# An expert layer's down product with weights stationary, its bias added by VectorE and its result transposed back by TensorE

## The chip, the core and the metric

The kernel runs on one core of a Trainium2 chip. A core has a matrix engine (TensorE; in the profile PE for its matmuls and PEld for its weight loads), VectorE (DVE), ScalarE (ACT), GpSimd (POOL) and SyncE (SP, which here issues DMAs). Each engine takes its own instructions in order, and they wait for one another by semaphores. TensorE multiplies a stationary operand, loaded as weights, with a moving one, and writes to PSUM, eight banks of 2 KB per partition; the other engines' data lie in SBUF, with 128 partitions. The metric is the device time of one execution in microseconds, lower being better.

## What is computed

Two layers, each with an attention and a mixture of experts, on 2 x 1024 tokens of 128 channels. The change lies in the experts of the first layer: a router picks one of 16 experts for each token, and the expert is a small two-layer network with biases.

```python
def _L0_ffn_ref(h, router_w, w1, b1, w2, b2):
    B, S, D, F, E = (2, 256, 128, 256, 16)
    b, s, d = h.shape
    x = h.reshape(-1, d)
    logits = x @ router_w
    assign = jnp.argmax(logits, axis=-1)
    w = jax.nn.sigmoid(jnp.take_along_axis(logits, assign[:, None], axis=1)[:, 0])
    hh = jnp.einsum('nd,edf->nef', x, w1) + b1
    hh = jax.nn.gelu(hh, approximate=False)
    all_out = jnp.einsum('nef,efd->ned', hh, w2) + b2
    out = jnp.take_along_axis(all_out, assign[:, None, None], axis=1)[:, 0, :]
    out = out * w[:, None]
    return out.reshape(b, s, d)
...
x = L0_attn_x
h = _layernorm(x, axis=-1) * (1 + ca) + sa
x = x + ga * _L0_attn_ref(h, ...)
h = _layernorm(x, axis=-1) * (1 + cb) + sb
x = x + gb * _L0_ffn_ref(h, ...)
...
```

The second layer (another attention, another set of experts) follows on `x`.

## The kernel before

The program has three phases, one after the other, with an exit of all engines between them: `rwkv_phase` (the first attention; it also routes the tokens and scatters their rows to `moe0_slots` in DRAM, sorted by expert), `expert_phase` (the experts of the first layer), and `layer1_phase`.

`expert_phase` works on 31 tiles of 128 rows: 16 that belong to one expert each and 15 more for rows that were over, whose expert is looked up. A tile goes through these steps:

- SyncE loads the rows (`xg`), TensorE transposes them into PSUM (`transpose`, L1453), and VectorE copies them to SBUF (`inputs`, L1422).
- TensorE makes the up product in two halves of 128 hidden units (`up`, L1462), weights stationary. The hidden units lie on the partitions, so ScalarE adds the first bias per partition as it applies the gelu (L1399) and writes `hid`.
- TensorE makes the down product (`down_product`). Before the change `hid` is the stationary operand and the weights move (L1469), so the tokens lie on the partitions of the result, as the store wants them. The second bias then varies along the free dimension; it is added by a third matmul, the bias column broadcast against the identity (L1471), accumulated into the same PSUM tile.
- VectorE copies the result from PSUM to `yg` (`results`, L1426), and SyncE stores `yg` to `moe0_slots` in eight groups of tiles (L1372), the last of three tiles. GpSimd waits for all stores and then gathers the first tokens' rows for the next phase (L1315).

All is written as a pipeline by hand: in round n TensorE transposes tile n+2, makes the up product of tile n and the down product of tile n-3; VectorE copies the inputs of tile n+2 and the results of tile n-3. Rounds run from -2 to 33, so the first rounds have no down product, rounds 29 and 30 no transpose, and the last three only a down product. A tile uses one of `DEPTH` = 8 PSUM banks: columns 0 to 255 hold the up product, 256 to 383 the transposed input (`tr`), 384 to 511 the down product (`down`). Tile n+8 may be transposed into a bank when the results of tile n have been copied.

After the loop TensorE runs 14 fillers (L1483) that keep it busy while the last results are stored; then each engine leaves the phase (L1322), and `layer1_phase` starts when all have.

Of the kernel before, what the change touches and what calls it, by code (L numbers as in the profile page):

```python
# [18 lines left out]
ALU = mybir.AluOpType  # L19
# [3 lines left out]
P = 128  # L23
# [15 lines left out]
E0, F0 = 16, 256  # L39
# [5 lines left out]
W0 = 2 * F0 + 3  # L45
# [66 lines left out]
def bass_adaln_stack(nc, t, out):  # L112

    ctx = ExitStack()
    with ctx:
# [64 lines left out]
        with nc.sbuf_tensor("hT_all", [P, TILES, P], F32) as hT_all:  # L180
            with nc.cleanup_on_exit():
                expert_phase(nc, t, const, bank + halves, cst, wall, s_wall, h_all, ends0, s_sent0, mx0,
                             gate, gate_rows, s_gate, yt, weight, slot0, s_back)
                layer1_phase(nc, t, const, x_sb, x_bc, eps_pow, sbw[:, 1], mod_col, mod_row, quad, bank, pair, cst,
                             hT_all, W1, s_w1, s_w2, s_fill, gate_rows, yt, weight, slot0, s_back, wall, h_all,
                             out)
# [1132 lines left out]
def expert_phase(nc, t, const, bank, cst, wall, s_wall, h_all, ends, s_sent, mx, gate,  # L1319
                 gate_rows, s_gate, yt, weight, slot, s_back):  # L1320

    with ExitStack() as ctx:  # L1322
        def sb(name, shape, dt=F32):
            return ctx.enter_context(nc.sbuf_tensor(name, shape, dt))

        def sem(name):
            return nc.alloc_semaphore(name)

        ALL = E0 + EXTRA0
        DEPTH = len(bank)  # L1330
# [9 lines left out]
        hid = [sb(f"e_hid{k}", [P, 2, P]) for k in range(DEPTH)]  # L1340
        yg = sb("e_yg", [P, ALL, C])
# [4 lines left out]
        s_out = sem("e_s_out")  # L1346
        e_xt, e_xc, e_up, e_gelu, e_down, e_y = (sem("e_s_xt"), sem("e_s_xc"), sem("e_s_up"), sem("e_s_gelu"),
                                                 sem("e_s_down"), sem("e_s_y"))
        s_grow, s_growc = sem("e_s_grow"), sem("e_s_growc")
        block = ctx.enter_context(nc.Block())  # L1350

        def tr(k):
            return bank[k][:, 2 * P:3 * P]

        def down(k):
            return bank[k][:, 3 * P:4 * P]

        def weights(n):
            return wall[:, n, :] if n < E0 else wdyn[:, n - E0, :]
# [42 lines left out]
        @block.vector  # L1402
        def _(dve):
            for k in range(len(BATCHES)):
                dve.tensor_tensor(le[:, :, k, :], ends[0:1, k, None, 1:].to_broadcast([1, EXTRA0, E0]),
                                  cst("iota15")[0:1, :, None].to_broadcast([1, EXTRA0, E0]), ALU.is_le).then_inc(s_step, 1)
            dve.wait_ge(s_step, len(BATCHES))
            dve.tensor_reduce(te[:, :], le[:, :, :, :].rearrange("p d k e -> p d (k e)"), AX.X, ALU.add)\
                .then_inc(s_step, 1)
            dve.wait_ge(s_step, len(BATCHES) + 1)  # L1410
            dve.tensor_copy(expert[:, :], te[:, :]).then_inc(s_step, 1)
            dve.wait_ge(s_step, len(BATCHES) + 2)
            dve.tensor_scalar(expert[:, :], expert[:, :], E0 - 1, None, ALU.bitwise_and).then_inc(s_tile, 1)

            dve.wait_ge(s_exp, 1)
            dve.tensor_scalar(weight[:, :], weight[:, :], 1.0, None, ALU.add).then_inc(s_exp, 1)
            dve.wait_ge(s_exp, 2)
            dve.reciprocal(weight[:, :], weight[:, :]).then_inc(s_exp, 1)

            def inputs(n):  # L1420
                dve.wait_ge(e_xt, n + 1)
                dve.tensor_copy(xgT[n % DEPTH][:, :], tr(n % DEPTH)).then_inc(e_xc, 1)  # L1422

            def results(n):
                dve.wait_ge(e_down, n + 1)
                dve.tensor_copy(yg[:, n, :], down(n % DEPTH)).then_inc(e_y, 1)  # L1426

            for n in range(-2, ALL + 3):
                if n + 2 < ALL:
                    inputs(n + 2)  # L1430
                if n >= 3:
                    results(n - 3)

        @block.tensor
        def _(pe):
            pe.wait_ge(s_gate, 16)
            for e in range(E1_LIVE):
                last = pe.matmul(bank[6][:, e * C:(e + 1) * C], gate[:, e:e + 1].to_broadcast([P, P]), cst("ident"),
                                 start=True, stop=True)
            last.then_inc(s_grow, 1)  # L1440
            for _ in range(3):
                pe.matmul(bank[5][:, 0:2 * P], cst("ident"), const[:, 0:2 * P], start=True, stop=True)

            def transpose(n):
                if n < E0:
                    pe.wait_ge(s_x[[b > n for _, b in LOADS].index(True)], 16)
                else:
                    pe.wait_ge(s_x[len(LOADS) + [b > n - E0 for _, b in OVER].index(True)], 16)
                if n >= DEPTH:
                    pe.wait_ge(e_y, n - DEPTH + 1)  # L1450
                if n == 6:
                    pe.wait_ge(s_growc, 1)
                pe.transpose(tr(n % DEPTH), xg[:, n, :], cst("ident")).then_inc(e_xt, 1)  # L1453

            def up(n):
                pe.wait_ge(e_xc, n + 1)
                if n == 0:
                    pe.wait_ge(s_wall, 16)
                if n >= E0:
                    pe.wait_ge(s_wt[n - E0], 16)  # L1460
                for f in range(2):
                    last = pe.matmul(bank[n % DEPTH][:, f * P:(f + 1) * P], weights(n)[:, f * P:(f + 1) * P],  # L1462
                                     xgT[n % DEPTH][:, :], start=True, stop=True)
                last.then_inc(e_up, 1)

            def down_product(n):
                pe.wait_ge(e_gelu, 2 * n + 2)
                for f in range(2):
                    pe.matmul(down(n % DEPTH), hid[n % DEPTH][:, f, :], weights(n)[:, F0 + f * P:F0 + (f + 1) * P],  # L1469
                              start=(f == 0), stop=False)  # L1470
                pe.matmul(down(n % DEPTH), weights(n)[:, W0 - 1:W0].to_broadcast([P, P]), cst("ident"), start=False,  # L1471
                          stop=True).then_inc(e_down, 1)

            for n in range(-2, ALL + 3):
                if n + 2 < ALL:
                    transpose(n + 2)
                if 0 <= n < ALL:
                    up(n)
                if n >= 3:
                    down_product(n - 3)  # L1480
            pe.wait_ge(e_y, ALL - 1)
            for _ in range(14):
                pe.matmul(bank[0][:, 0:2 * P], cst("ident"), const[:, 0:2 * P], start=True, stop=True)  # L1483
# [1128 lines left out]
```

## Time and profile before

| | us |
|---|---|
| median of 3 runs | 685.11 (685.09 to 685.81) |
| the profiled execution | 684.28 |
| its span in the profile | 682.2 |
| of it, the loop over the expert tiles from round 4 on | 204.29 to 239.19 |
| TensorE busy in the span | 641.0 (94%) |
| VectorE busy | 421.7 (62%) |
| ScalarE busy | 302.7 (44%) |
| GpSimd busy | 254.8 (37%) |

The span is the time from the first to the last instruction of the profiled execution; 2.1 us of the execution lie around it. Times inside the profile are counted from the start of the span. A busy TensorE is not one at its peak, since its matmuls overlap and their ends are modelled: the distance from one weight load to the next tells its pace better. An instruction's idle time before it, with what ended it, stands in square brackets in the rows below.

### The profile page before, as it was taken

What the parts mean: (1) busy time and instruction counts of PE and PEld (TensorE: products, weight loads), DVE (VectorE), ACT (ScalarE), POOL (GpSimd) and SP (SyncE); (2) the same over time, 40 slices, a digit from 0 to 9 for tenths busy, and PEclk for the clock granted to TensorE, in tenths of its full rate; (3) what the DMA queues carried; (4) which work ended last, traced back from release to release, by engine and by line L of the source; (5) the groups of instructions that cost most, each with busy time, mean ns of one, the idle gap of its engine ahead of it and who ended that gap; (6) DMA issues with size and microseconds to landing.
All of it is one profiled execution on the core that took longest, in us unless ns stands there. A gap on an engine that the chain in (4) does not pass through costs nothing.

```text
span 682.2 us, 26441 instructions
## 1 busy us (share of the span) xinstructions
PE 641.0 (94%) x10978; PEld 547.5 (80%) x10978; DVE 421.7 (62%) x1384; ACT 302.7 (44%) x1017; POOL 254.8 (37%) x387
## 2 busy tenths in 40 slices
PE   5899999999759989999999999999999999999995
PEld 4567777777649977888888888888887999989995
DVE  3777777777633326577777686868676554444442
ACT  1456666643025414545545554545454353333331
POOL 1455666556710031131525252524243432322325
PEclk9899999999969999999999999999999999999999
DMA  7899200000048210000000000000221667566462
GB/s 191 287 299 308 57 3 2 4 6 19 25 137 244 82 43 7 7 9 7 20 12 20 14 18 16 16 16 12 97 77 26 225 223 240 186 214 225 154 241 62
DMA packets 50486, 65.69 MB, mean 96 GB/s; under 512 B 5168, under 2 KB 40208, under 8 KB 47424
## 3 DMA queue, kind: packets, MB, share of 16 engines
q1 hardware_dynamic: 44992, 57.22, 26.8%
q0 software_dynamic: 2912, 6.03, 2.6%
q8 instruction: 88, 1.44, 0.9%
q10 hardware_dynamic: 2464, 0.76, 0.5%
q14 instruction: 30, 0.25, 0.1%
HBM read 49.45 MB, written 18.87 MB: 100 GB/s over the span
## 4 chain that ended last, share of the span: by engine, by line
PE 59%; DVE 2%; DMA 1%; ACT 1%; issue 0%; SPq 0%; DVEq 0%
PE bank L1924 7%; PE quad L1782 6%; PE quad L1906 6%; PE quad L1908 5%; PE bank L1807 4%; PE pair L1744 3%; PE bank L1830 3%; PE quad L1788 2%; PE pair L1746 2%; PE pair L1745 2%; PE bank L1840 2%; PE pair L1769 2%; PE bank L1843 2%; PE bank L1833 2%; PE bank L1926 1%; PE quad L1911 1%
## 5 line engine op out<-in xcount | busy, mean ns | idle before, releaser
L2183 DVE TENSOR_TENSOR h_masked<-quad,const 128x1536 f32<-128x1536 f32 (+2 forms) x66 | 112.6, 1706 | 59.9 <-PE quad L1788 54.1
L2021 ACT ACTIVATE f_sa<-quad 128x256 f32<-128x256 f32 (+1 forms) x115 | 40.3, 352 | 91.6 <-PE quad L1908 75.8
L2202 DVE TENSOR_TENSOR f_hid<-f_sa,quad 128x256 f32<-128x256 f32 (+1 forms) x115 | 43.1, 380 | 53.6 <-ACT f_sa L2021 53.5
L2403 POOL DMA_INDIRECT moe_slots<-g_pay,g_slot x28 | 28.9, 1034 | 77.2 <-PE bank L1852 68.7
L1924 PE MATMUL bank<-wall,f_hid 128*128 128x128 f32 x390 | 50.7, 277 | 1.1 <-DVE f_hid L2205 0.9
L1924 PEld LDWEIGHTS bank<-wall,f_hid 128*128 128x128 f32 x390 | 47.8, 192 | 3.6 <-DVE f_hid L2205 2.8
L1906 PE MATMUL quad<-f_xT,wall 128*128 128x256 f32 (+1 forms) x190 | 50.0, 345 | 0.5 <-DVE f_hid L2202 0.5
L1908 PE MATMUL quad<-f_xT,wall 128*128 128x256 f32 (+1 forms) x190 | 49.2, 341 | 0.0
L1998 ACT ACTIVATE h_gT<-bank 128x128 f32<-128x128 f32 x64 | 17.8, 278 | 66.2 <-PE bank L1833 66.2
L1782 PE MATMUL quad<-h_qk 32*128 32x128 f32 x1024 | 46.5, 296 | 0.3 <-DVE h_masked L2183 0.3
L1782 PEld LDWEIGHTS quad<-h_qk 32*128 32x128 f32 x1024 | 34.3, 185 | 9.5 <-issue 7.0
L1807 PE MATMUL bank<-h_qk,h_state 32*32 32x128 f32 x1024 | 40.9, 274 | 0.0
L1972 ACT ACTIVATE h_qk<-pair 128x256 f32<-128x256 f32 x64 | 24.6, 384 | 36.1 <-PE pair L1746 36.1
L2483 POOL DMA_INDIRECT moe_out<-f_y,f_token x31 | 30.3, 977 | 23.9 <-DVE f_y L2311 16.5
L837 POOL TENSOR_TENSOR kl<-kl,tot 128x128 f32<-128x128 f32 x56 | 25.1, 449 | 33.6 <-DVE state L725 10.6
L1132 PE MATMUL bank<-const 128*128 128x256 f32 x134 | 35.1, 398 | 0.9 <-DVE sbw L479 0.9
L1908 PEld LDWEIGHTS quad<-f_xT,wall 128*128 128x128 f32 x190 | 33.4, 191 | 3.1
L1906 PEld LDWEIGHTS quad<-f_xT,wall 128*128 128x128 f32 x190 | 31.4, 191 | 3.5 <-issue 1.0
L1744 PE MATMUL pair<-hT_all,hla_wq 128*128 128x128 f32 x128 | 29.8, 315 | 0.7 <-ACT h_vt L1974 0.7
L1807 PEld LDWEIGHTS bank<-h_qk,h_state 32*32 32x32 f32 x1024 | 23.7, 104 | 7.7
L1981 ACT ACTIVATE h_kqt<-pair 128x256 f32<-128x256 f32 x64 | 24.8, 387 | 9.3 <-PE pair L1769 9.3
L1132 PEld LDWEIGHTS bank<-const 128*128 128x128 f32 x134 | 24.2, 194 | 4.2 <-DVE mod_row L471 1.3
(414 smaller groups left out, 1791.2 us busy)
## 6 DMA issues: line engine op xcount, KB each, us to landing
wall<-moe_w SPq DMA_DIRECT2D x23, 1088.0 KB, 5.1
moe_slots<-blank SPq DMA_DIRECT2D x2, 2112.0 KB, 24.4
wall<-in_experts_dram SPq DMA_DIRECT2D x1, 4120.0 KB, 21.8
e_w<-in_experts_dram SPq DMA_DIRECT2D x15, 257.5 KB, 3.3
moe_slots<-blank SPq DMA_DIRECT2D x1, 1984.0 KB, 9.7
moe_slots<-e_yg SPq DMA_DIRECT2D x7, 256.0 KB, 3.7
f_xg<-moe_slots SPq DMA_DIRECT2D x12, 132.0 KB, 4.1
moe_w<-in_moe_w_dram SPq DMA_DIRECT2D x1, 1408.0 KB, 7.2
```

The source lines that it names most:

```text
L1132: pe.matmul(bank[of][:, 0:N], cst("ident"), const[:, 0:N], start=True, stop=True)
L1744: pe.matmul(proj[:, 0:P], W["q"][:, cols], hT, start=True, stop=True)
L1782: last = pe.matmul(quad[:, h, a * P:(a + 1) * P], qk[q][head(h), 1 - a, :], qk[q][head(h), a, :], start=True, stop=True, tile_position=(h ...
L1807: pe.matmul(left[head(h), part * P:(part + 1) * P], states[k][head(h), (0 if part else 2 * D):(D if part else 3 * D)], qk[k][head(h), 1 - ...
L1906: pe.matmul(up_bank(n, f)[:, 0:s], w[:, F1 + TAIL1 + f * P:F1 + TAIL1 + (f + 1) * P], x_of(n)[:, 0:s], start=True, stop=True)
L1908: pe.matmul(up_bank(n, f)[:, T1:T1 + s], w[:, f * P:(f + 1) * P], x_of(n)[:, 0:s], start=True, stop=True).then_inc(f_up, 1)
L1924: pe.matmul(acc[k], hid[n % 2][:, f, cols], w[:, 2 * F1 + f * C:2 * F1 + (f + 1) * C], start=(f == 0), stop=False)
L2021: act.activation(sa[g % 3][:, 0:s], up_bank(n, f)[:, 0:s], ACT.Silu).then_inc(f_sa, 1)
L2183: dve.tensor_tensor(masked[k % 4][:, :, a * P:z * P], quad[:, :, a * P:z * P], cst("causal")[:, None, a * P:z * P].to_broadcast([P, HPG, ( ...
L2202: dve.tensor_tensor(hid[n % 2][:, f, 0:s], sa[g % 3][:, 0:s], up_bank(n, f)[:, T1:T1 + s], ALU.mult)\
L2403: pool.indirect_dma_start(out=t["moe1_slots"], out_offset=bass.IndirectOffsetOnAxis(ap=slot[:, b * 2 + k:b * 2 + k + 1], axis=0), in_=pay[ ...
L2483: pool.indirect_dma_start(out=t["moe1_out"], out_offset=bass.IndirectOffsetOnAxis(ap=token_of[n % 2][:, k:k + 1], axis=0), in_=yg[n % 2][: ...
```

## The change

The operands of the down product change places: the weights are stationary and `hid` moves, so the result has the output channels on the partitions and the tokens along the free dimension. The third matmul goes away. VectorE adds the second bias per partition as it takes the result out of PSUM (`biased`, into one of three buffers `yT`), TensorE transposes that back (`turn`) into the columns 0 to 127 of the same bank, which the up product has left, and VectorE copies it to `yg` as before. Two semaphores are new. The loops have one more round: in round n TensorE turns tile n-4 ahead of the down product of tile n-3, and VectorE copies the results of tile n-4 ahead of the bias of tile n-3.

```diff
--- before.py
+++ after.py
@@ -1346,6 +1346,8 @@
         s_out = sem("e_s_out")
         e_xt, e_xc, e_up, e_gelu, e_down, e_y = (sem("e_s_xt"), sem("e_s_xc"), sem("e_s_up"), sem("e_s_gelu"),
                                                  sem("e_s_down"), sem("e_s_y"))
+        yT = [sb(f"e_yT{k}", [P, P]) for k in range(3)]
+        e_biased, e_turned = sem("e_s_biased"), sem("e_s_turned")
         s_grow, s_growc = sem("e_s_grow"), sem("e_s_growc")
         block = ctx.enter_context(nc.Block())
 
@@ -1354,6 +1356,9 @@
 
         def down(k):
             return bank[k][:, 3 * P:4 * P]
+
+        def turned(k):
+            return bank[k][:, 0:P]
 
         def weights(n):
             return wall[:, n, :] if n < E0 else wdyn[:, n - E0, :]
@@ -1421,15 +1426,24 @@
                 dve.wait_ge(e_xt, n + 1)
                 dve.tensor_copy(xgT[n % DEPTH][:, :], tr(n % DEPTH)).then_inc(e_xc, 1)
 
+            def biased(n):
+                dve.wait_ge(e_down, n + 1)
+                if n >= 3:
+                    dve.wait_ge(e_turned, n - 2)
+                dve.tensor_scalar(yT[n % 3][:, :], down(n % DEPTH), weights(n)[:, W0 - 1:W0], None, ALU.add)\
+                    .then_inc(e_biased, 1)
+
             def results(n):
-                dve.wait_ge(e_down, n + 1)
-                dve.tensor_copy(yg[:, n, :], down(n % DEPTH)).then_inc(e_y, 1)
-
-            for n in range(-2, ALL + 3):
+                dve.wait_ge(e_turned, n + 1)
+                dve.tensor_copy(yg[:, n, :], turned(n % DEPTH)).then_inc(e_y, 1)
+
+            for n in range(-2, ALL + 4):
                 if n + 2 < ALL:
                     inputs(n + 2)
-                if n >= 3:
-                    results(n - 3)
+                if n >= 4:
+                    results(n - 4)
+                if 3 <= n < ALL + 3:
+                    biased(n - 3)
 
         @block.tensor
         def _(pe):
@@ -1466,17 +1480,22 @@
             def down_product(n):
                 pe.wait_ge(e_gelu, 2 * n + 2)
                 for f in range(2):
-                    pe.matmul(down(n % DEPTH), hid[n % DEPTH][:, f, :], weights(n)[:, F0 + f * P:F0 + (f + 1) * P],
-                              start=(f == 0), stop=False)
-                pe.matmul(down(n % DEPTH), weights(n)[:, W0 - 1:W0].to_broadcast([P, P]), cst("ident"), start=False,
-                          stop=True).then_inc(e_down, 1)
-
-            for n in range(-2, ALL + 3):
+                    last = pe.matmul(down(n % DEPTH), weights(n)[:, F0 + f * P:F0 + (f + 1) * P],
+                                     hid[n % DEPTH][:, f, :], start=(f == 0), stop=(f == 1))
+                last.then_inc(e_down, 1)
+
+            def turn(n):
+                pe.wait_ge(e_biased, n + 1)
+                pe.transpose(turned(n % DEPTH), yT[n % 3][:, :], cst("ident")).then_inc(e_turned, 1)
+
+            for n in range(-2, ALL + 4):
                 if n + 2 < ALL:
                     transpose(n + 2)
                 if 0 <= n < ALL:
                     up(n)
-                if n >= 3:
+                if n >= 4:
+                    turn(n - 4)
+                if 3 <= n < ALL + 3:
                     down_product(n - 3)
             pe.wait_ge(e_y, ALL - 1)
             for _ in range(14):
```

In the rows below an instruction is given as its line, its operation, the tile that it writes, those that it reads (the moving one first), and the shape; "x2" is two of them. `quad`, `pair`, `bank6` and `bank7` are PSUM. First TensorE in the middle of the loop, two rounds, before: L1453 is the transpose, L1462 the up product, L1469 and L1471 the down product and its bias.

```order
L1453 MATMUL quad<-const,e_xg 128x128
L1462 MATMUL quad<-e_xgT1,e_w 128x128 x2
L1469 MATMUL pair<-e_w,e_hid6 128x128 x2
L1471 MATMUL pair<-const,e_w 128x128
L1453 MATMUL bank6<-const,e_xg 128x128
L1462 MATMUL quad<-e_xgT2,e_w 128x128 x2
L1469 MATMUL pair<-e_w,e_hid7 128x128 x2
L1471 MATMUL pair<-const,e_w 128x128
```

The same two rounds on TensorE after: L1467 is the transpose, L1476 the up product, L1489 the turn, L1483 the down product.

```order
L1467 MATMUL quad<-const,e_xg 128x128
L1476 MATMUL quad<-e_xgT1,e_w 128x128 x2
L1489 MATMUL bank7<-const,e_yT0 128x128
L1483 MATMUL pair<-e_hid6,e_w 128x128 x2
L1467 MATMUL bank6<-const,e_xg 128x128
L1476 MATMUL quad<-e_xgT2,e_w 128x128 x2
L1489 MATMUL pair<-const,e_yT1 128x128
L1483 MATMUL pair<-e_hid7,e_w 128x128 x2
```

The bias matmul after the down product is gone; between the up product and the down product stands the turn of the tile whose down product ended the round before.

TensorE at the end of the loop, before (L1483 here is the fillers):

```order
L1462 MATMUL pair<-e_xgT6,e_w 128x128 x2
L1469 MATMUL quad<-e_w,e_hid3 128x128 x2
L1471 MATMUL quad<-const,e_w 128x128
L1469 MATMUL bank6<-e_w,e_hid4 128x128 x2
L1471 MATMUL bank6<-const,e_w 128x128
L1469 MATMUL bank7<-e_w,e_hid5 128x128 x2
L1471 MATMUL bank7<-const,e_w 128x128
L1469 MATMUL pair<-e_w,e_hid6 128x128 x2
L1471 MATMUL pair<-const,e_w 128x128
L1483 MATMUL quad<-const 128x256 x14
```

And after (the fillers are L1502):

```order
L1476 MATMUL pair<-e_xgT6,e_w 128x128 x2
L1489 MATMUL quad<-const,e_yT2 128x128
L1483 MATMUL quad<-e_hid3,e_w 128x128 x2
L1489 MATMUL quad<-const,e_yT0 128x128
L1483 MATMUL bank6<-e_hid4,e_w 128x128 x2
L1489 MATMUL bank6<-const,e_yT1 128x128
L1483 MATMUL bank7<-e_hid5,e_w 128x128 x2
L1489 MATMUL bank7<-const,e_yT2 128x128
L1483 MATMUL pair<-e_hid6,e_w 128x128 x2
L1489 MATMUL pair<-const,e_yT0 128x128
L1502 MATMUL quad<-const 128x256 x14
```

Down products and turns alternate, each turn directly behind the down product of its own tile, and one more turn stands at the end.

VectorE at the same place, before (L1422 copies inputs, L1426 results):

```order
L1426 COPY e_yg<-pair 128x128
L1422 COPY e_xgT5<-bank7 128x128
L1426 COPY e_yg<-quad 128x128
L1422 COPY e_xgT6<-pair 128x128
L1426 COPY e_yg<-quad 128x128 x3
L1426 COPY e_yg<-bank6 128x128
```

And after (L1427 copies inputs, L1438 turned results, L1433 adds the bias):

```order
L1427 COPY e_xgT5<-bank7 128x128
L1438 COPY e_yg<-pair 128x128
L1433 TENSOR_SCALAR e_yT0<-quad,e_w 128x128
L1427 COPY e_xgT6<-pair 128x128
L1438 COPY e_yg<-quad 128x128
L1433 TENSOR_SCALAR e_yT1<-quad,e_w 128x128
L1438 COPY e_yg<-quad 128x128
L1433 TENSOR_SCALAR e_yT2<-quad,e_w 128x128
```

A bias add has come into each round, behind the copy of the tile before it.

## Rows read from the trace of the kernel before

**Rows 1.** Busy us by stretch: length, TensorE, weight loads, VectorE, ScalarE, GpSimd, granted clock, DMA.

```profile
204.29:234.94 30.65, 30.65 (x278) 30.65 (x276) 12.21 (x50) 15.66 (x52) 0.00 (x0) 1.00 0.64 185
234.94:237.18 2.24, 2.24 (x23) 2.24 (x22) 0.58 (x2) 1.26 (x6) 0.00 (x0) 1.00 0.01 3
237.18:239.19 2.01, 2.01 (x21) 2.01 (x20) 0.88 (x3) 0.26 (x2) 0.00 (x0) 1.00 0.23 68
```

**Rows 2.** Order of time in one round: start us, us of the group, engine, instruction.

```profile
215.88 0.53 PEld L1469 LDWEIGHTS quad<-wall,e_hid 128*128 128x128 f32 x4
...
216.33 0.30 PEld L1471 LDWEIGHTS quad<-const,wall 128*128 128x128 f32 x2
...
216.55 0.14 PEld L1453 LDWEIGHTS quad<-const,e_xg 128*128 128x128 f32 x1
...
216.86 0.29 DVE L1426 COPY e_yg<-quad 128x128 f32<-128x128 f32 x1 [0.74 <-PE quad L1471]
217.07 0.28 DVE L1422 COPY e_xgT<-quad 128x128 f32<-128x128 f32 x1
```

**Rows 3.** Order of time, the first round with a down product.

```profile
203.63 0.53 PEld L1469 LDWEIGHTS quad<-wall,e_hid 128*128 128x128 f32 x4
...
204.07 0.30 PEld L1471 LDWEIGHTS quad<-const,wall 128*128 128x128 f32 x2
```

**Rows 4.** Order of time, the end of the loop.

```profile
238.96 0.30 PEld L1471 LDWEIGHTS pair<-const,e_w 128*128 128x128 f32 x2
...
239.19 0.73 PEld L1483 LDWEIGHTS quad<-const 128*128 128x128 f32 x4
...
239.49 0.29 DVE L1426 COPY e_yg<-pair 128x128 f32<-128x128 f32 x1 [0.38 <-PE pair L1471]
239.81 0.36 SPq L1372 DMA_DIRECT2D moe_slots<-e_yg  x1
```

**Rows 5.** Order of time from the last store to layer 1.

```profile
242.12 0.99 POOL L1315 DMA_INDIRECT e_yt<-moe_slots,slot_of_token  x1 [49.07 <-DMA moe_slots<-e_yg]
...
246.30 0.35 DVE L2040 SCALAR_TENSOR_TENSOR e_yt<-e_yt,router_weight,mod_row 128x128 f32<-128x128 f32 x1 [6.51 <-PEq L1322]
```

**Rows 6.** The exits of two engines: count, duration ns, start us.

```profile
L1322 PEldq DRAIN  x1: 4050/4050/4050, 241.5 to 241.5; - x1
L1322 POOLq DRAIN  x1: 4117/4117/4117, 241.9 to 241.9; - x1
```

**Rows 7.** VectorE by line and shape: count, busy us, mean ns, idle before.

```profile
L2311 DVE TENSOR_SCALAR f_y<-bank,f_xg 128x128 f32<-128x128 f32 x31 | 10.8, 350 | 21.5 <-PE bank L1926 21.5
...
L2057 DVE TENSOR_SCALAR p_xn<-x_sb,p_mv,p_rstd 128x128 f32<-128x128 f32 x16 | 4.9, 366 | 3.2 <-POOL p_rstd L2364 3.1 <-DVE g_cum L2067 0.2
L1426 DVE COPY e_yg<-quad 128x128 f32<-128x128 f32 x16 | 4.7, 292 | 12.1 <-PE quad L1471 12.1
```

**Rows 8.** Order of time at two hand-overs from VectorE to TensorE in layer 1.

```profile
301.12 0.48 DVE L2075 BATCH_NORM_STATS2 g_st<-x_sb 128x6 f32<-128x128 f32 x2
...
301.69 0.12 PEld L1807 LDWEIGHTS bank<-h_qk,h_state 32*32 32x32 f32 x4
...
566.57 0.41 DVE L2205 TENSOR_TENSOR f_hid<-f_sa,quad 64x256 f32<-64x256 f32 x1
...
567.03 0.19 PEld L1924 LDWEIGHTS bank<-wall,f_hid 128*128 128x128 f32 x1 [0.22 <-DVE f_hid L2205]
```

**Rows 9.** TensorE alone by stretch: length, busy us, granted clock, DMA share, GB/s.

```profile
198.20:200.90 2.70, 2.70 (x8) 0.50 0.94 273
...
244.00:248.00 4.00, 2.13 (x10) 1.00 0.07 21
```

**Rows 10.** Fillers by line and shape: count, busy us, mean ns of one.

```profile
L1483 PE MATMUL quad<-const 128*128 128x256 f32 x28 | 6.2, 379 | 0.0
...
L1442 PE MATMUL bank<-const 128*128 128x256 f32 x6 | 2.8, 634 | 0.0
```

## The prediction

> **What bounds the kernel now.** I read the busy times by stretch first. From 204.29 to 239.19 us, the loop over the 31 expert tiles, TensorE is busy all the time at a granted clock of 1.00; VectorE and ScalarE are busy 12.2 and 15.7 us of the first 30.65 [rows 1]. TensorE is what limits this stage. The 25 full rounds of the loop (a transpose, an up product, a down product with its bias) take 30.65 us, 1.226 us each. A round has 11 TensorE records: 1 of the transpose, 4 of the up product, 4 of the down product, 2 of the bias (a float32 matmul leaves two records, a transpose one), and so a record takes **p = 0.1115 us**. Then come two rounds without a transpose, 2.24 us, and three of down product and bias alone, 2.01 us [rows 1].
>
> Second, the order of time inside a round. The weight loads follow one another without a gap: down product at 215.88, bias at 216.33, next transpose at 216.55. The second load of the bias therefore stands at 216.33 + p = 216.44, and VectorE starts to copy the result at 216.86: **0.42 us** from the last weight load of a product to the start of the operation that reads it [rows 2]. At the end of the loop it is the same: 238.96 + p = 239.07, and the copy starts at 239.49 [rows 4]. Today this delay costs TensorE nothing, because nothing on TensorE waits for what VectorE made of a result, except a transpose several rounds later.
>
> Third, what follows. The last copy (239.49) lets SyncE store the last three tiles (239.81), the landing lets GpSimd gather (242.12), and layer 1 starts on VectorE at 246.30, when all engines have left the expert phase [rows 4, 5]. GpSimd leaves at 241.9 + 4.1 = 246.0, TensorE, behind its fillers, at 241.5 + 4.05 = 245.5 [rows 6]. So the end of the loop is on the path that sets the end, by way of GpSimd, and TensorE's fillers are 0.5 us behind. I see nothing later that starts by itself and could take up a shift: DMA engines are busy 7% of the time from 244 to 248 us [rows 9], and the gathers, the residual and the projections hang on one another.
>
> **The change, part by part.** *Operands of the down product exchanged*: 4 records as before, now of the up product's form (weights stationary, activations moving); both have pitch p inside the same rounds [rows 1, 2], so 0. A tile's down product comes three rounds after its up product, so the wait for its gelus stays met.
>
> *Bias matmul out, turn in.* Two records go, one transpose record comes, p less per tile: 31 x 0.1115 = 3.46 us, if TensorE never waited. That is the most the change can give.
>
> *New wait.* Now TensorE's turn of a tile needs the biased tile from VectorE, and VectorE needs the down product. Between the last load of the down product of a tile and the load of its turn lie: 0.42 us until VectorE starts [rows 2]; the bias add; and the hand-over to TensorE's weight load. The bias add is a VectorE TENSOR_SCALAR of 128x128 float32 from PSUM with a scalar per partition; the kernel has exactly this form in layer 1, 31 times at **0.350 us**, while a plain copy takes 0.292 [rows 7]. The hand-over from VectorE to a waiting weight load: the instruction that began at 566.57 and took 0.41 ended at 566.98, the load started at 567.03: **0.05 us** [rows 8]. Together L = 0.42 + 0.35 + 0.05 = **0.82 us**. The bias add has a second wait (its buffer, a turn three tiles older), long met.
>
> The Trainium skill, "VectorE: DVE Perf Modes", in the section on the TRN2 errata, gives one cost for any VectorE operation from PSUM to SBUF (120 cycles and one per element at 0.96 GHz, an estimate of 0.258 us here), and its table of perf modes puts copy and scalar operation into one row. By it the bias add would cost what a copy costs; the rows show 0.350 against 0.292, and I go by the rows. With the page's 0.258 us the sum below would be about +0.8 us instead of +3.7.
>
> What lies under L? TensorE goes in order: after the down product of a tile it does the next round's transpose (p) and up product (4p), then comes to the turn. That is 6p = 0.67 us from the last load of the down product, so in a full round it waits 0.82 - 0.67 = 0.15 us. And behind the waiting turn stands the next down product, on which the next turn hangs. That closes a loop: turn, down product, result to VectorE, bias, back to the turn. Its length is p for the turn's load, 3p to the last load of the down product after it, and L: **4p + 0.82 = 1.266 us per tile**, whatever else is in the round. It holds for the rounds without a transpose and, above all, for the last three, in which there is nothing to lie under the wait.
>
> VectorE can follow: 0.28 + 0.29 + 0.35 = 0.92 us per round [rows 2, 7]. It takes the copy of the turned tile 0.42 us after the turn's load and is done by 0.71; the next bias add can't start before 3p + p + 0.42 = 0.87. So the bias add isn't queued behind a copy. Transposes wait for copies two rounds older, and slack remains. ScalarE's load per tile stays, with more time for it. The weight loads of SyncE's queue only get more time; its stores are late as the results are.
>
> **The sum.** The first down product starts where it did, 203.63, its last load at 203.63 + 3p = 203.96 [rows 3]; there is no turn in that round. Before, the last bias load of tile 0 came 2p = 0.22 us later and that of tile 30 34.90 us after that (30.65 + 2.24 + 2.01), at 239.07. Now the turn of tile 0 is loaded at 203.96 + 0.82 = 204.78 and that of tile 30 at 204.78 + 30 x 1.266 = 242.76. Piece by piece: tile 0, 0.82 - 0.22 = +0.60; 25 full rounds, each 0.04 longer, +1.00; two rounds without transpose, 2.53 for 2.24, +0.29; three last rounds, 3.80 for 2.01, +1.79. **Together +3.7 us.** The saved record is in it already; the wait takes it back in each round, and the drained end costs 1.8 us on top. From there both are alike: copy 0.42 us after the load, store, gather, exit. TensorE's fillers wait for the copy of the last tile but one, met by then, and start 3.7 us later as well.
>
> The profiled execution took 684.28 us (span 682.2), which would become 688.0. The median of the runs is 685.11, 0.8 above it; I forecast **688.8 us**, +0.54%.
>
> Bounds: the bias add between the copy's 0.29 and the 0.37 of the dearest VectorE scalar operation of this size [rows 7]; the hand-over between 0.05 and the 0.09 of another, from 301.12 + 0.48 to 301.69 [rows 8]. L counts 31 times (30 rounds and tile 0). Low: 31 x 0.06 less, +1.8. High: 31 x 0.06 more, +5.6. A gain is excluded as long as L stays over 0.70 (below).
>
> **Rivals.**
> 1. *The wait is covered, TensorE alone sets the pace* (not slower). It decides by L: if L is at most 6p = 0.67, each round is 10p = 1.115 us to the end, tile 30 is turned at 203.96 + 0.67 + 30 x 1.115 = 238.08, and the change is 238.08 - 239.07 = -1.0 us: 684.1. Break-even is L = 0.70. For it: all three terms come from other instructions than the new ones. Against it: the 0.42 us is seen at every tile, and with 0.05 for the hand-over the bias add would have to take 0.23 us, less than any copy of that size [rows 7]. Chance 0.06 with what lies between.
> 2. *The clock falls* (slower still). In the last rounds TensorE has 5 records in 1.266 us, 0.56 us of load pitch, for about 4 us. If that counts as too little, the fillers run at 1.2 GHz: records of the same form have a mean of 634 ns at clock 0.50 and 379 at 1.00, with a pitch of (2.8 - 0.63)/5 = 0.43 against (6.2 - 0.38)/27 = 0.216 us [rows 9, 10]; 28 x 0.21 = 5.9 us, less the 0.5 us of slack: 694.2. Against: from 244.00 to 248.00 TensorE is busy 2.13 of 4 us, and the clock stays 1.00 there [rows 9]. Chance 0.04. The Trainium skill, "TensorE: Matmul & The Clock Gate", Part 4 on the PE-mode transpose, says that transposes don't engage the full clock as matmuls do, and one record in five would be one here; in the trace the loop with one in eleven stays at 1.00 [rows 1], which decides nothing for one in five.
> 3. *The shift is swallowed behind the loop.* If something else than the last copy released layer 1, TensorE's or GpSimd's exit would be late by less: 685.1. Against: GpSimd's gather waits for the landing of the store, and its exit is the last [rows 5, 6]. Chance 0.03.
>
> **How the numbers follow.** Forecast 0.87, rivals 0.06, 0.04, 0.03. The range is that of the forecast's bounds, 685.11 + 1.8 = 686.9 to 685.11 + 5.6 = 690.7; outside lie the rivals, 13 in 100, and a little of the forecast's own tails. A measurement of this kernel can tell about 0.2%, 1.4 us, from no change. Slower by more than that: the forecast and rival 2, 0.91. Within: rival 3 and most of rival 1, 0.07. Faster by more: it would need nearly all waits hidden, 0.02.
>
> **What would show it.** In the profile after: bias adds of 0.35 us; the weight load of the turn idle before it, released by VectorE, some 0.15 us in full rounds, 0.26 in the two without a transpose and 0.7 in the last; tiles 1.27 us apart from the first to the last, ends included; the last copy of results at 243.2; layer 1 from about 250.0, and after that everything shifted alike. TensorE busy without a gap, and tiles 1.115 us apart, would mean rival 1. A granted clock of 0.50 about 240 to 250 us would mean rival 2. If the last copy is late and layer 1 isn't, it is rival 3.

## The result, and the profile after

| | before | after |
|---|---|---|
| median of 16 runs, us | 686.75 (685.09 to 689.77) | 689.53 (687.93 to 694.3) |
| ratio after / before | | 1.0053, 95% interval 1.0035 to 1.0070 |
| profiled execution, us | 684.28 | 688.47 |
| its span, us | 682.2 | 686.4 |
| last weight load of the first down product to the start of the last copy of results, us | 35.53 | 37.80 |

The change makes the kernel slower by 0.5%, which is what was forecast (688.8 us, range 686.9 to 690.7). By the interval it costs 2.4 to 4.8 us. (The 16 runs of before hold the 3 that the forecast started from. The ratios with an interval, here and below, are not quotients of the medians beside them, which here would be 1.0040.) The last row of the table is the stretch that the change acts on. I call it M and use it for every kernel below, because it repeats to 0.01 us where totals spread over several us. It is read from two rows of the order of time: the start of the first down product's weight loads plus 3p (p = 0.1115 us, the prediction's pitch of a record), and the start of the last copy. Before it goes from 203.96 [rows 3] to 239.49 [rows 4]. The sum of the prediction would have made it 39.2.

The first stretch of M after the change, in order of time on all engines (start us, us of the group, engine, instruction, idle time before it and its releaser):

```profile
204.18 0.53 PEld L1483 LDWEIGHTS quad<-e_hid,wall 128*128 128x128 f32 x4
...
204.94 0.35 DVE L1433 TENSOR_SCALAR e_yT<-quad,wall 128x128 f32<-128x128 f32 x1 [0.60 <-PE quad L1483]
...
205.34 0.14 PEld L1489 LDWEIGHTS quad<-const,e_yT 128*128 128x128 f32 x1
205.34 0.33 PE L1489 MATMUL quad<-const,e_yT 128*128 128x128 f32 x1
205.34 0.58 PEld L1483 LDWEIGHTS quad<-e_hid,wall 128*128 128x128 f32 x4
```

The down product of tile 0 ends its loads at 204.18 + 0.33 = 204.51; VectorE takes the result 0.42 us later (0.43 between these rounded rows), its bias add ends at 205.29, and 0.05 us after that the turn is loaded. The way from a down product to its turn therefore took 205.34 - 204.51 = 0.83 us, where L = 0.82 had been worked out.

Busy time by stretch after, in the columns of [rows 1]: the 25 full rounds, the two without a transpose, the drained end up to the last turn, and the 6.3 us behind it:

```profile
204.62:235.12 30.50, 30.50 (x252) 28.54 (x251) 20.85 (x75) 15.88 (x52) 0.00 (x0) 1.00 0.67 189
235.12:237.34 2.22, 2.22 (x18) 1.84 (x17) 1.16 (x4) 1.14 (x5) 0.00 (x0) 1.00 0.36 104
237.34:242.06 4.72, 2.94 (x21) 2.18 (x20) 2.58 (x8) 0.39 (x2) 0.00 (x0) 1.00 0.19 56
242.06:248.40 6.34, 6.26 (x29) 5.19 (x29) 0.29 (x1) 0.00 (x0) 1.94 (x2) 1.00 0.18 52
```

The full rounds take 30.50 us, against 30.65 before, with one record less in each and 2 us of idle weight loads in all (28.54 of 30.50). VectorE's busy time went from 12.21 to 20.85 us. The drained end, 2.01 us before, is now 4.72 us long and TensorE is busy for 2.94 of them. The granted clock is 1.00 everywhere.

Two rounds in the middle of the loop after:

```profile
215.10 0.14 PEld L1489 LDWEIGHTS quad<-const,e_yT 128*128 128x128 f32 x1
...
215.10 0.58 PEld L1483 LDWEIGHTS quad<-e_hid,wall 128*128 128x128 f32 x4
...
215.47 0.29 DVE L1438 COPY e_yg<-quad 128x128 f32<-128x128 f32 x1 [0.22 <-PE quad L1489]
...
215.60 0.14 PEld L1467 LDWEIGHTS pair<-const,e_xg 128*128 128x128 f32 x1
...
215.92 0.35 DVE L1433 TENSOR_SCALAR e_yT<-quad,wall 128x128 f32<-128x128 f32 x1 [0.16 <-PE quad L1483]
...
216.32 0.14 PEld L1489 LDWEIGHTS quad<-const,e_yT 128*128 128x128 f32 x1
```

From turn to turn it is 1.22 us, and so it is for all 31 tiles (1.219 to 1.223), in the full rounds, in the two without a transpose, and in the last ones. And the end of the loop:

```profile
239.50 0.14 PEld L1489 LDWEIGHTS bank<-const,e_yT 128*128 128x128 f32 x1 [0.64 <-DVE e_yT L1433]
...
240.73 0.14 PEld L1489 LDWEIGHTS bank<-const,e_yT 128*128 128x128 f32 x1 [0.64 <-DVE e_yT L1433]
...
241.94 0.14 PEld L1489 LDWEIGHTS pair<-const,e_yT 128*128 128x128 f32 x1 [0.64 <-DVE e_yT L1433]
...
242.31 0.29 DVE L1438 COPY e_yg<-pair 128x128 f32<-128x128 f32 x1 [0.42 <-PE pair L1489]
...
244.93 0.99 POOL L1315 DMA_INDIRECT e_yt<-moe_slots,slot_of_token  x1 [50.50 <-DMA moe_slots<-e_yg]
...
249.48 0.61 DVE L2059 SCALAR_TENSOR_TENSOR e_yt<-e_yt,router_weight,mod_row 128x128 f32<-128x128 f32 x2 [6.87 <-PEq L1322]
```

There the weight loads stand idle for 0.64 us before each turn, released by VectorE. The last copy starts 2.82 us later than before (242.31 against 239.49 [rows 4]), the gather 2.81 us later, layer 1 on VectorE 3.18 us later [rows 5]. Of this, 0.55 us was there when the loop began (204.51 against 203.96 [rows 3]); of the 0.36 us that came in between the gather and layer 1, 0.10 is left at the last attention block.

The profiled executions differ by 4.19 us: 0.55 at the loop's entry, 2.27 in M, 0.10 from the last copy to the last attention block of layer 1, and 1.27 in the last stage, behind that block. The 2.27 us lie where the prediction looked. The first and the last of these four are taken up again under e4 to e6 and e8.

### The profile page after: what moved, and what is told of

Its sections match the earlier page's. It is cut to its first block, busy times and chain, and to the rows that moved or that the text cites. A ratio compares the mean times of both kernels' runs of the same rounds, so it can differ in the third digit from the quotient of the medians.

```text
span 686.4 us, 26438 instructions
## 1 busy us (share of the span) xinstructions
PE 641.5 (93%) x10947; PEld 543.9 (79%) x10947; DVE 431.9 (63%) x1415; ACT 302.6 (44%) x1017; POOL 254.4 (37%) x387
## 4 chain that ended last, share of the span: by engine, by line
PE 59%; DVE 2%; DMA 1%; ACT 1%; issue 0%; SPq 0%; DVEq 0%
PE bank L1943 6%; PE quad L1801 6%; PE quad L1925 6%; PE quad L1927 5%; PE bank L1826 4%; PE pair L1763 3%; PE bank L1849 3%; PE quad L1807 2%; PE pair L1765 2%; PE pair L1764 2%; PE bank L1859 2%; PE pair L1788 2%; PE bank L1862 2%; PE bank L1852 2%; PE bank L1945 1%; PE quad L1930 1%
```

## The experiments

Two questions stayed open: whether the closed loop (turn, next down product, bias add, turn) is what costs the time, and why a tile takes 1.22 us instead of 1.27.

**The order of turn and down product.** In e1 TensorE makes the next down product first and the turn of the tile before after it; VectorE adds the bias before it copies.

```diff
-                if n >= 4:
-                    results(n - 4)
                 if 3 <= n < ALL + 3:
                     biased(n - 3)
+                if n >= 4:
+                    results(n - 4)
...
-                if n >= 4:
-                    turn(n - 4)
                 if 3 <= n < ALL + 3:
                     down_product(n - 3)
+                if n >= 4:
+                    turn(n - 4)
```

> Edit: TensorE takes the down product of tile n-3 ahead of the turn of tile n-4 in each round, and VectorE the bias of tile n-3 ahead of the copy of tile n-4. All instructions and all waits stay. Measure: M, from the last weight load of the first down product to the start of the last copy of results; 35.53 us in the kernel before, 37.79 in the changed one. Theory A (the loop turn, next down product, bias, next turn sets 1.22 us per tile, because the next down product stands behind the waiting turn): the wait of 0.826 us now has a transpose, an up and a down product under it, so full rounds fall to 10 records, 1.115 us, with no idle time at the turn; only the last three rounds and the last turn wait. M = 32.8 us, 2.7 less than before; total 2.7 us under the kernel before (ratio 0.996). Rival B (VectorE's third operation per tile, or the PSUM banks that it shares with TensorE, limits the tiles to 1.22 us): rounds stay at 1.22, M about 37.5, total as the changed kernel (ratio 1.004).

M (forecast 32.8) became 32.66 us, 2.87 us less than before the change and 5.14 less than after. Order of time: the first down product, one round from turn to turn, the last turn, the last copy:

```profile
203.95 0.53 PEld L1483 LDWEIGHTS quad<-e_hid,wall 128*128 128x128 f32 x4
...
215.40 0.14 PEld L1489 LDWEIGHTS quad<-const,e_yT 128*128 128x128 f32 x1
...
215.51 0.14 PEld L1467 LDWEIGHTS quad<-const,e_xg 128*128 128x128 f32 x1
...
215.71 0.35 DVE L1433 TENSOR_SCALAR e_yT<-quad,wall 128x128 f32<-128x128 f32 x1 [0.37 <-PE quad L1483]
...
216.51 0.14 PEld L1489 LDWEIGHTS quad<-const,e_yT 128*128 128x128 f32 x1
...
236.57 0.14 PEld L1489 LDWEIGHTS pair<-const,e_yT 128*128 128x128 f32 x1 [0.42 <-DVE e_yT L1433]
...
236.94 0.29 DVE L1438 COPY e_yg<-pair 128x128 f32<-128x128 f32 x1 [0.23 <-PE pair L1489]
```

In the full rounds the turns are 1.11 us apart, ten records of p, and no weight load waits before one; at the drained end some do, the last one 0.42 us. The total is 683.81 us (681.31 to 688.44, 12 runs), against 689.85 for the kernel before on the same chip (29 runs): ratio 0.9943, interval 0.9911 to 0.9975. The same instructions, with two operations exchanged on each of the two engines, turn the loss into a gain, so the loss is the wait, and not what the added operations cost. No run exchanges them on one engine alone; but in the rows after the change the bias add itself stood idle before it started, until TensorE released it (0.16 us at 215.92), so VectorE's order was not what held it up.

**The size of the bias add.** In e2 a plain copy stands in place of the bias add, so the second bias is left out.

```diff
-                dve.tensor_scalar(yT[n % 3][:, :], down(n % DEPTH), weights(n)[:, W0 - 1:W0], None, ALU.add)\
-                    .then_inc(e_biased, 1)
+                dve.tensor_copy(yT[n % 3][:, :], down(n % DEPTH)).then_inc(e_biased, 1)
```

> Edit: the changed kernel with the bias add replaced by a plain copy; the second bias is left out, nothing else. Theory A: the bias add stands in the loop once per tile, so its 0.058 us (0.350 less 0.292) come off each of the 31 links: tiles 1.162 us apart, M = 37.79 - 31 x 0.058 = 36.0 us. Rival B (throughput of VectorE): a round's VectorE work falls from 0.92 to 0.86 us, so the same sign, but it would have been VectorE that is busy without a pause, which a share of 75% doesn't show. Rival C (the rounds are set by TensorE's records and the wait is a by-product): tiles stay 1.22 us apart.

```profile
211.01 0.53 PEld L1482 LDWEIGHTS quad<-e_hid,wall 128*128 128x128 f32 x4
...
222.20 0.29 DVE L1433 COPY e_yT<-quad 128x128 f32<-128x128 f32 x1 [0.16 <-PE quad L1482]
...
222.54 0.14 PEld L1488 LDWEIGHTS quad<-const,e_yT 128*128 128x128 f32 x1
...
223.70 0.14 PEld L1488 LDWEIGHTS quad<-const,e_yT 128*128 128x128 f32 x1
...
247.25 0.29 DVE L1437 COPY e_yg<-pair 128x128 f32<-128x128 f32 x1 [0.42 <-PE pair L1488]
```

The copy is 0.06 us shorter, the tiles are 1.16 us apart instead of 1.22, and M is 35.91. What VectorE takes is passed on, once per tile, as it must be if it lies in the loop. (The total, 693.88 us of a single run, tells nothing: this execution entered the loop 7 us later than that of after.)

**The drained end.** In e3 the last three tiles are made as before the change, with the bias matmul and no turn; the loops (not shown) call `direct` for these tiles and end a round earlier.

```diff
+        TURNED = ALL - 3
...
+            def direct(n):
+                dve.wait_ge(e_down, n + 1)
+                dve.tensor_copy(yg[:, n, :], down(n % DEPTH)).then_inc(e_y, 1)
...
+                if n >= TURNED:
+                    for f in range(2):
+                        pe.matmul(down(n % DEPTH), hid[n % DEPTH][:, f, :],
+                                  weights(n)[:, F0 + f * P:F0 + (f + 1) * P], start=(f == 0), stop=False)
+                    pe.matmul(down(n % DEPTH), weights(n)[:, W0 - 1:W0].to_broadcast([P, P]), cst("ident"),
+                              start=False, stop=True).then_inc(e_down, 1)
+                    return
...
```

> Edit: the changed kernel, with the last three tiles (28 to 30) done as in the kernel before: hidden units stationary, bias matmul, result copied straight out; the order of the rest as changed. It prices the drained end alone. Theory A: the first 28 tiles stay 1.22 us apart; then the last three rounds fall from 1.22 to 0.67 us and no turn is left behind the last down product. M = 36.1 us, 1.65 less than changed, 0.6 more than before; total 0.6 us over the kernel before (within what can be told). Rival D (the whole loss lies in the steady rounds): M stays about 37.5.

```profile
206.94 0.53 PEld L1497 LDWEIGHTS quad<-e_hid,wall 128*128 128x128 f32 x4
...
241.07 0.14 PEld L1503 LDWEIGHTS quad<-const,e_yT 128*128 128x128 f32 x1 [0.63 <-DVE e_yT L1434]
...
242.24 0.30 PEld L1493 LDWEIGHTS bank<-const,e_w 128*128 128x128 f32 x2
...
242.91 0.30 PEld L1493 LDWEIGHTS pair<-const,e_w 128*128 128x128 f32 x2
...
243.45 0.29 DVE L1443 COPY e_yg<-pair 128x128 f32<-128x128 f32 x1 [0.38 <-PE pair L1493]
```

One turn still waits 0.63 us; behind it the tiles are 0.67 us apart again (242.24 to 242.91). M is 36.18, which is 1.62 us less than after: the drained end's share of the loss. What is left is 0.65 us. The total is 690.0 us (686.2 to 694.11, 12 runs), ratio to before 1.0019, interval 0.9988 to 1.0049, so nothing can be told from no change.

**Both.** e4 has e1's order and e3's end; its edits are those two.

> Edit: both at once: the turn behind the next down product, and the last three tiles as in the kernel before. Theory A: 28 tiles save one record each and no wait is left anywhere on TensorE: M = 32.4 us, 3.1 under the kernel before; total 3.1 us under it (ratio 0.9955), 0.4 under the turn-behind kernel. Rival B: rounds stay at 1.22 us, M about 36.

```profile
211.16 0.53 PEld L1497 LDWEIGHTS quad<-e_hid,wall 128*128 128x128 f32 x4
...
242.07 0.14 PEld L1503 LDWEIGHTS quad<-const,e_yT 128*128 128x128 f32 x1
242.18 0.53 PEld L1491 LDWEIGHTS bank<-e_w,e_hid 128*128 128x128 f32 x4
...
243.83 0.29 DVE L1443 COPY e_yg<-pair 128x128 f32<-128x128 f32 x1 [0.38 <-PE pair L1493]
```

M is 32.34 us, the shortest of the kernels that compute everything: 3.19 us less than before. The total is 686.82 (683.32 to 689.92, 12 runs), ratio 0.9947, interval 0.9919 to 0.9974. Between e1 and e4 the totals can't choose: their M differ by 0.32 us, which is 0.05% of the time.

This profile entered the loop at 211.49 us, 7.5 us later than that of before, with the same program ahead of the loop. The granted clock differs there. TensorE alone in the first 100 us (length, busy us, granted clock, DMA share, GB/s), first before:

```profile
0.00:50.00 50.00, 36.70 (x405) 0.93 0.85 256
50.00:100.00 50.00, 49.74 (x771) 1.00 0.52 135
```

and e4:

```profile
0.00:50.00 50.00, 38.75 (x332) 0.80 0.89 270
50.00:100.00 50.00, 48.01 (x767) 0.93 0.53 121
```

With 1.2 and 2.4 GHz as the two levels, before spent some 7 us of the first 100 at the lower one (1.00 less 0.93 is 0.07, twice that of 50 us), e4 some 27 us. Over all ten profiles the loop's entry goes with this time: 7 us gives 203.96, 14 gives 204.28 (e1) and 204.51 (after), 17 to 21 give 206.2 to 207.3, and 27 give 211.0 to 211.5; the kernel before alone entered at 203.96 and, in e5 below, at 206.85. Whether the lower clock makes the loop late, or what makes it late lowers the clock, no run tells.

**Is the rest of the difference the change's?** After, e1, e2, e3 and e4 all showed 165.6 to 166.1 us from the last attention block to the end of the span, before 164.35. GpSimd waits there for a transfer of routed results; its add by line (count, busy us, mean ns, idle before and releaser), before and after:

```profile
L2497 POOL TENSOR_TENSOR e_yt<-e_yt 128x896 f32<-128x896 f32 x1 | 2.1, 2076 | 13.2 <-DMA e_yt<-moe_out 13.2
```

```profile
L2516 POOL TENSOR_TENSOR e_yt<-e_yt 128x896 f32<-128x896 f32 x1 | 2.1, 2074 | 14.4 <-DMA e_yt<-moe_out 14.4
```

If the change's buffers and semaphores had caused these 1.2 us, they would be part of its price. So e5 is the kernel before once more, unchanged, and e6 is that kernel with the change's buffers and semaphores but no use of them.

```diff
+        yT = [sb(f"e_yT{k}", [P, P]) for k in range(3)]
+        e_biased, e_turned = sem("e_s_biased"), sem("e_s_turned")
```

> Edit: none, the kernel before, for a second profile. The changed kernel's profile and those of its four variants are 1.2 to 1.7 us longer than the first profile of before between the last attention block and the end (165.6 to 166.1 against 164.3 us); in each of them the load of the routed results takes 8.5 us to reach GpSimd, in that profile 7.4. Theory E (chance, the load's time varies from one execution to the next): a second profile of before may show 8.5 us as well. Rival F (the change causes it, by the two semaphores or the three buffers that it takes): before shows 7.4 again, 164.3 us to the end.

> Edit: the kernel before, with the change's two semaphores and three buffers taken and not used. Theory E: its end, from the last attention block on, has no relation to the spare ones; 164.3 or 165.6 us as the execution before it by chance. Rival F: 165.6 us here and 164.3 in the plain second profile. The loop is that of before in either case: M = 35.5 us.

M was 35.53 us in both, as in the first profile of before. The last stage took 163.71 and 163.68 us, with GpSimd waiting 13.1 and 13.3 us, so spare buffers cost nothing there; and e8 below, which has all the change's buffers, semaphores and instructions, had 163.86 and this row:

```profile
L2517 POOL TENSOR_TENSOR e_yt<-e_yt 128x896 f32<-128x896 f32 x1 | 2.1, 2082 | 13.2 <-DMA e_yt<-moe_out 13.2
```

The longer wait is not something that the change must bring. e1 to e4 ran on one chip and all had it (14.5 or 14.6 us); e5 to e8 ran on another and none had it (13.1 to 13.3 us), with or without the change. What brings it about, no run shows. The totals of e5 and e6, 686.52 and 686.02 us, are single runs.

**What the loop passes on.** e7 exchanges the operands as the change does, drops the bias matmul, and neither adds the bias nor turns the result: two records less per tile and no wait.

```diff
-                    pe.matmul(down(n % DEPTH), hid[n % DEPTH][:, f, :], weights(n)[:, F0 + f * P:F0 + (f + 1) * P],
-                              start=(f == 0), stop=False)
-                pe.matmul(down(n % DEPTH), weights(n)[:, W0 - 1:W0].to_broadcast([P, P]), cst("ident"), start=False,
-                          stop=True).then_inc(e_down, 1)
+                    last = pe.matmul(down(n % DEPTH), weights(n)[:, F0 + f * P:F0 + (f + 1) * P],
+                                     hid[n % DEPTH][:, f, :], start=(f == 0), stop=(f == 1))
+                last.then_inc(e_down, 1)
```

> Edit: the kernel before with the operands of the down product exchanged and the bias matmul left out; results are copied out as they lie. The second bias and the turning back are left out. It prices the exchange alone, and shows whether the loop's end passes on to the total. Theory A (an exchanged matmul costs what it did): 9 records in a full round, 1.003 us, 8 in the next two, 4 in the last three: M = 253 x 0.1115 + 0.42 = 28.6 us, 6.9 under before, and the total falls by as much (ratio 0.990). Rival G (the exchange has a price of its own, as waiting longer for the hidden units that now move): M over 29.5. Rival H (something behind the loop takes up part of a shift): M 28.6, total less than 5 us under before.

```profile
205.89 0.53 PEld L1469 LDWEIGHTS quad<-e_hid,wall 128*128 128x128 f32 x4
...
216.36 0.14 PEld L1453 LDWEIGHTS quad<-const,e_xg 128*128 128x128 f32 x1
...
217.36 0.14 PEld L1453 LDWEIGHTS quad<-const,e_xg 128*128 128x128 f32 x1
...
234.83 0.29 DVE L1426 COPY e_yg<-pair 128x128 f32<-128x128 f32 x1 [0.15 <-PE pair L1469]
```

A round takes 1.00 us, nine records of p, so the exchange of operands costs nothing. M is 28.61 us, 6.92 less than before. The total is 679.74 (678.8 to 680.22, 4 runs), ratio 0.9899, interval 0.9883 to 0.9916, which on 685.91 us is 5.8 to 8.0 us less. So the third rival (the shift swallowed behind the loop) falls: by the interval, at least 5.8 of the 6.9 us that the loop saved reached the end. Whether all of it did is open. In the profiles e7 took 0.57 us more than e5 from the last copy to the last attention block (278.87 against 278.30) and 0.69 more behind it (164.40 against 163.71); e7's second layer works on other values, and whether that is why, no run shows.

**Why 1.22 and not 1.27.** After the change, the down product's first load starts 4 ns after that of the turn (both 215.10 above), where loads elsewhere in the loop are p apart. Either this belongs to the transpose, or to any load after a wait. In e8 the turn is an ordinary matmul against the identity, of two records.

```diff
-                pe.transpose(turned(n % DEPTH), yT[n % 3][:, :], cst("ident")).then_inc(e_turned, 1)
+                pe.matmul(turned(n % DEPTH), yT[n % 3][:, :], cst("ident"), start=True, stop=True)\
+                    .then_inc(e_turned, 1)
```

> Edit: the changed kernel with the turn as an ordinary float32 matmul against the identity, two records for one. In the changed kernel the time from the load of a turn that waited to the last load of the down product behind it is 0.394 us; the sum had 4p = 0.446. Theory I (the short restart comes with the transpose, whose load is short, 0.14 against 0.19 us): with a matmul the five records take their full pitch, 0.55 us, and tiles come 0.826 + 0.55 = 1.38 us apart, M = 0.83 + 30 x 1.38 + 0.42 = 42.6 us. Rival J (any first record after a wait is 0.05 us cheaper): 1.33 us apart, M = 41.1.

```profile
210.67 0.53 PEld L1483 LDWEIGHTS quad<-e_hid,wall 128*128 128x128 f32 x4
...
215.97 0.30 PEld L1489 LDWEIGHTS quad<-const,e_yT 128*128 128x128 f32 x2
216.18 0.53 PEld L1483 LDWEIGHTS bank<-e_hid,wall 128*128 128x128 f32 x4
...
217.35 0.30 PEld L1489 LDWEIGHTS bank<-const,e_yT 128*128 128x128 f32 x2
...
253.73 0.29 DVE L1438 COPY e_yg<-pair 128x128 f32<-128x128 f32 x1 [0.58 <-PE pair L1489]
```

Here the loads keep their pitch after the wait: the down product begins 0.21 us after the turn's first of two loads. The tiles are 1.38 us apart: from the turn's second load (0.108 us after the first) to the next turn it is 1.271 us, the prediction's 4p + 0.82 = 1.266 almost to the letter. M is 42.73 us. So the short restart belongs to this transpose behind a wait, and not to the wait alone; whether to its being a transpose or to its having one record, e8 does not separate. The total of the one run was 698.36 us, with the loop entered at 211.0.

## Why the prediction was right, point by point

**The bound.** TensorE set the pace of the loop and the loop's end set the start of layer 1, as the prediction read it from [rows 1] and [rows 5, 6]. e7 shows it from the other side: 6.9 us out of the loop are 5.8 to 8.0 us out of the total.

**The wait.** L was put together from three rows of other instructions and came to 0.82; measured it is 0.826, at each of the 31 tiles. The bias add itself, by line after:

```profile
L1433 DVE TENSOR_SCALAR e_yT<-quad,wall 128x128 f32<-128x128 f32 x8 | 2.8, 351 | 1.7 <-PE quad L1483 1.7
```

It takes 0.351 us, as the same form took in layer 1 [rows 7]. The Trainium skill, "VectorE: DVE Perf Modes", in its section on the TRN2 errata, gives one cost for both, by estimate 0.258 us (120 cycles and one per element at 0.96 GHz); here the scalar operation took 0.351 and the copy 0.292 (e2), so the measurement decides against it. Bounds that had been left for the add and the hand-over were not needed. The idle time forecast before the turn (0.15, 0.26 and 0.7 us) reads in the rows as 0.08, 0.19 and 0.64 (30.50 less 28.54 over 25 rounds, 2.22 less 1.84 over two, and the last rows). The wait is the one forecast, since 0.826 less 6p is 0.157; the idle time is some 0.08 us shorter because a load ahead of the turn takes 0.19 us and not p.

**The closed loop.** All 31 tiles are equally far apart, ends included, as the prediction said they would be. e1, in which the turn stands behind the next down product, breaks the loop and gets the rhythm of the first rival (10p = 1.115 us, measured 1.11). So that rival's arithmetic was sound; its condition, L of 0.67 or less, didn't hold (0.826). In e1 the turn comes one more down product later and the 0.83 us are covered in the full rounds.

**The term that was mis-sized** is "p for the turn's load, 3p to the last load of the down product after it", 4p = 0.446 us. It measured 0.394 after the change: the next load starts 4 ns after that of the turn, the others follow 0.166, 0.112 and 0.112 us apart (the next transpose is loaded p behind the last of them, at 215.60, 0.50 us after the turn). A tile so takes 0.394 + 0.826 = 1.220 us, not 1.266, and 30 rounds of it account for 1.4 us of the sum. A smaller miss is the step to the copy, "copy 0.42 us after the load": behind a turn that waited it was 0.37 us (241.94 to 242.31), which takes 0.05 us off the end of M. Piece by piece, forecast and measured:

| | forecast us | measured us |
|---|---|---|
| tile 0 | +0.60 | +0.60 |
| 25 full rounds | +1.00 | -0.15 |
| two rounds without transpose | +0.29 | +0.20 |
| three last rounds | +1.79 | +1.65 |
| together, to the last turn | +3.7 | +2.3 |

In the full rounds the saved record and the wait cancel (1.220 against 1.226 us before). The whole loss of the loop lies at its ends, where nothing covers the wait; e3, which takes the drained end back, confirms that share with 1.62 us.

**The total.** The medians differ by 2.78 us, and 688.8 was forecast where 689.53 was measured. That the two lie so close is luck. The forecast added its 3.7 us to a median of 685.11 (3 runs), and the median of before over 16 runs is 686.75, 1.64 us higher; added to that, the sum would have given 690.4. A start too low and a price too high made up for each other. The loop gave 2.27 us where 3.7 were expected, and the way from it to the last attention block another 0.10; these 2.4 us lie at the low end of the interval (2.4 to 4.8). The pair of profiled executions differs by 0.55 us more at the loop's entry and 1.27 in the last stage. The prediction had looked at neither, and e5, e6 and e8 show that the change need not bring the second. Whether the median holds some of the change beyond 2.4 us, these runs don't settle.

**The clock.** The second rival falls: through the drained end, TensorE busy 2.94 of 4.72 us, and through the fillers after it the granted clock stays at 1.00 (stretches above). The Trainium skill, "TensorE: Matmul & The Clock Gate", Part 4, says that transposes don't engage the full clock; the trace has one in five records a transpose there and the clock didn't fall, so the page's rule took nothing from this kernel. With four matmul records to each transpose, the runs don't test the rule further.

## What to carry to other kernels

When an in-order engine must wait for another engine's answer, look at what stands right behind the wait: if it is the instruction that starts the next round trip, the round trip becomes the period of the loop (here 0.83 us of latency and 0.39 of work per tile), and one operation fewer buys nothing. Issue the next question before waiting for the last answer; exchanging two operations on each of two engines was worth 5.1 us of the loop here and made the kernel 0.6% faster than before (interval 0.25 to 0.9%). And cost the drained end by itself, at the full latency, since nothing is left to lie under it.

## What the runs showed of the hardware

- The turn, a transpose that had waited for its operand, let the next weight load start 4 ns after its own (up to 14 ns in e2, where the wait is shorter), and the five loads from it on took 0.394 us from first to last; after a wait that ended in an ordinary matmul, the loads went on 0.108 us apart (e8).
- The hand-over from VectorE's end to a waiting weight load is 0.05 us, and from the last weight load of a down product to VectorE's start 0.42 us, at each of the 31 tiles. From the one load of a turn that waited to VectorE's start it is 0.37 us.
- The time that the chip spends at the lower clock in the first 100 us differs from execution to execution (7 to 27 us in ten profiles), and the loop's entry goes with it, by up to 7.5 us. That is three times the effect studied here, while M repeats to 0.01 us (before, e5 and e6).
